# Four ring banks for the projections, one shared bank for all transposes, and a later split of a group's first weight chunk

## What is computed

```python
x = layernorm(x + mixer(x, ...))        # x is (16, 128, 256)
x = layernorm(x + xattn(x, ctx, ctx))   # 32 query heads, 8 key heads of size 8
x = layernorm(x + moe(x, ...))          # 8 experts, top 2, and a shared one

def mixer(x, W_in, conv_w, conv_b, A_log, D_param, dt_bias, W_out):
    proj = x @ W_in.T
    val, gate, Bp, Cp, dt = split(proj)      # 512, 512, 32*128, 32*128, 32
    val = silu(causal_conv(val, conv_w) + conv_b)
    dt = softplus(dt + dt_bias); ld = dt * -exp(A_log)
    # per head h: Y = (C B^T * exp(cum_l - cum_m), causal) @ val + D * val
    Y = Y * silu(gate)
    return Y @ W_out.T
```

## Time and profile before

| | us |
|---|---|
| median of 3 runs | 813.26 |
| lowest and highest | 808.52, 814.21 |
| the profiled execution, its own time | 812.88 |
| its span in the profile | 811.1 |

### The profile page before, as it was taken

How to read it: one execution, slowest core, us unless ns; L and a number is a source line. 1 busy time by engine, 2 the same in 40 slices (tenths; PEclk the granted TensorE clock), 3 DMA queues, 4 the chain that set the end, 5 groups by cost and what they waited for, 6 DMA issues and landing times. The chain is left out here.

```text
span 811.1 us, 17004 instructions
## 1 busy us (share of the span) xinstructions
PE 738.9 (91%) x5786; PEld 401.0 (49%) x5791; DVE 598.5 (74%) x1037; ACT 432.8 (53%) x781; POOL 370.0 (46%) x408
## 2 busy tenths in 40 slices
PE   6699999999999999999999999997799998686673
PEld 2355565555655555555555565665134443333342
DVE  4578767687686786776767778885788898449995
ACT  5665445754444664544575544554277887532333
POOL 5466337463453583433749637633023212115672
PEclk9799999999999999999999999999699999798997
DMA  7355421227423132542223533220230000034401
GB/s 262 97 168 169 104 51 54 65 50 126 134 52 87 43 78 52 168 103 49 54 58 84 98 72 67 62 45 1 95 112 22 21 22 21 0 127 167 151 26 52
DMA packets 35509, 66.28 MB, mean 82 GB/s; under 512 B 7121, under 2 KB 12113, under 8 KB 33873
## 3 DMA queue, kind: packets, MB, share of 16 engines
q1 hardware_dynamic: 34896, 65.28, 30.0%
q10 hardware_dynamic: 576, 0.56, 0.2%
HBM read 62.49 MB, written 2.42 MB: 80 GB/s over the span
## 5 line engine op out<-in xcount | busy, mean ns | idle before, releaser
L280 POOL TENSOR_TENSOR cum_rows<-cum_rows,cum_t 128x512 f32<-128x512 f32 x128 | 136.4, 1076 | 195.4 <-DMA cum_rows<-cum_scratch 195.4
L758 PE MATMUL pring<-xt_hi,w_hi 128*128 (+1 forms) x576 | 173.5, 383 | 11.5 <-DVE conv_h L647 6.8
L758 PE MATMUL pring<-xt_lo,w_hi 128*128 (+1 forms) x576 | 172.8, 382 | 0.0
L758 PE MATMUL pring<-xt_hi,w_lo 128*128 (+1 forms) x576 | 172.7, 382 | 0.0
L626 DVE TENSOR_TENSOR bt<-pring,bt 128x512 f16<-128x512 f32 x128 | 88.1, 688 | 74.1 <-ACT bt L434 74.0
L434 ACT CAST bt<-pring 128x512 f16<-128x512 f32 x128 | 74.6, 583 | 116.8 <-PE pring L758 116.8
L630 DVE TENSOR_TENSOR ct<-pring,ct 128x512 f16<-128x512 f32 x128 | 88.2, 689 | 55.6 <-ACT ct L438 55.3
L797 PEld LDWEIGHTS pscore<-ct,bt 128*128 128x128 f16 x1536 | 95.9, 98 | 34.7 <-issue 7.2
L797 PE MATMUL pscore<-ct,bt 128*128 128x128 f16 x1536 | 106.7, 219 | 2.9 <-DVE mt L598 2.2
L438 ACT CAST ct<-pring 128x512 f16<-128x512 f32 x128 | 74.8, 584 | 54.8 <-PE pring L758 54.8
L1089 DVE TENSOR_REDUCE mx<-bank_at 128x4 f32<-128x512 f32 x128 | 83.5, 689 | 14.0 <-PE bank_at L1165 13.0
(11 more groups left out here) (154 smaller groups left out, 944.2 us busy)
## 6 DMA issues: line engine op xcount, KB each, us to landing
cum_rows<-cum_scratch SPq DMA_DIRECT2D x32, 1024.0 KB, 8.0
w_raw<-in_w_in SPq DMA_DIRECT2D x34, 256.0 KB, 7.1
weight_b<-weight_scratch SPq DMA_DIRECT2D x8, 1024.0 KB, 6.5
q_rows<-in_xt SPq DMA_DIRECT2D x4, 512.0 KB, 6.1
acc<-in_x SPq DMA_DIRECT2D x1, 2048.0 KB, 7.6
vals<-in_vals SPq DMA_DIRECT2D x16, 128.0 KB, 2.0
out<-acc SPq DMA_DIRECT2D x4, 512.0 KB, 2.9
w_raw_e<-in_w_up SPq DMA_DIRECT2D x1, 1024.0 KB, 4.8
```

Source lines behind the costliest of these rows:

```text
L280: nc.gpsimd.tensor_tensor(rows[:, par, :, q], rows[:, par, :, q], own, ALU.subtract).then_inc(sem("since"), 1)
L758: mm = nc.tensor.matmul(bank[name][:], w[:, c, k, cols], x[:, k, bass.ds(n % TB, 1), :].rearrange("p o n -> p (o n)"), start=(i == 0), sto ...
```

## The change

The ring of three banks becomes one of four. T leaves the ring: the transposed values, the turned sums and all turned queries share a new bank, `pturn`, and `pdt` becomes another name of `py`. `turn_sums` of the later token blocks now waits for `pad_values(0)`, `turn_values` of step 15 for the queries of step 14, and `turn_q(b)` waits for `evac_q(b - 1)` where it waited for `evac_q(b - 2)`. In a refill step, `hi_part(refill, 0)` moves behind `evac_b(n, 0)`, `evac_c(n, 0)` and `decays(n, 0)`. No instruction of work is added or removed.

```diff
--- before.py
+++ after.py
@@ -123,23 +123,25 @@
         stats = sb("stats0", [P, NB, 6], F32)
         block_mv = sb("block_mv0", [P, NB, 2], F32)
 
-        pring = [ps(f"pring{i}", [P, TOK]) for i in range(3)]
+        RING = 4
+        pring = [ps(f"pring{i}", [P, TOK]) for i in range(RING)]
         pscore = [ps(f"pscore{i}", [P, TOK]) for i in range(2)]
-        pcum = ps("pcum", [P, TB, NB, H])
+        pturn = ps("pturn", [P, TOK])
+        pcum = pturn[:].rearrange("p (t b h) -> p t b h", t=TB, b=NB)
         py = ps("py", [P, TOK])
-        pdt = ps("pdt", [P, TOK])
-        turned = [pcum[:].rearrange("p t b h -> p (t b h)").bitcast(F16).rearrange("p (i n) -> p i n", n=L),
-                  pdt[:].bitcast(F16).rearrange("p (i n) -> p i n", n=L)]
-
-
-        order = ["val", "gate", "B0", "C0", "B1", "C1", "B2", "C2", "O0", "O1", "B3", "C3", "T"]
+        pdt = py
+        turned = pturn[:].bitcast(F16).rearrange("p (i n) -> p i n", n=L)
+
+
+        order = ["val", "gate", "B0", "C0", "B1", "C1", "B2", "C2", "O0", "O1", "B3", "C3"]
         order += [f"{k}{s}" for s in range(4, SLOTS) for k in "BC"]
-        bank = {name: pring[i % 3] for i, name in enumerate(order)}
-        assert len(order) % 3 == 0
+        bank = {name: pring[i % RING] for i, name in enumerate(order)}
+        assert len(order) % RING == 0
+        bank["T"] = pturn
 
         def consumed(eng, name, n):
 
-            i = order.index(name) - 3
+            i = order.index(name) - RING
             m = n if i >= 0 else n - 1
             was = order[i % len(order)]
             if was == "val":
@@ -150,10 +152,8 @@
                 eng.wait_ge(sem("b_evac"), 8 * m + int(was[1]) + 2)
             elif was[0] == "C":
                 eng.wait_ge(sem("c_evac"), 8 * m + int(was[1]) + 3)
-            elif was[0] == "O":
+            else:
                 eng.wait_ge(sem("acc_add"), 2 * m + int(was[1]) + 1)
-            else:
-                eng.wait_ge(sem("val_pad"), m + 2)
 
         mean_var, rstd, expo = moments
 
@@ -439,7 +439,7 @@
 
             def evac_q(b):
                 act.wait_ge(sem("q_turn_mm"), b + 1)
-                nc.scalar.copy(q_rows[:, b].rearrange("p t g n -> p (t g) n"), turned[b % 2]).then_inc(sem("q_rows"), 1)
+                nc.scalar.copy(q_rows[:, b].rearrange("p t g n -> p (t g) n"), turned).then_inc(sem("q_rows"), 1)
 
             def silus(n):
                 act.wait_ge(sem("gate_proj"), n + 1)
@@ -482,11 +482,11 @@
 
             def step(n, refill=None, queries=()):
                 silus(n)
-                if refill is not None:
-                    hi_part(refill, 0)
                 evac_b(n, 0)
                 evac_c(n, 0)
                 decays(n, 0)
+                if refill is not None:
+                    hi_part(refill, 0)
                 evac_b(n, 1)
                 high_y(n)
                 if refill is not None:
@@ -782,6 +782,8 @@
             def turn_sums(t0, t1):
                 if t0 == 0:
                     pe.wait_ge(sem("in_early"), 48)
+                else:
+                    pe.wait_ge(sem("val_pad"), 2)
                 for t in range(t0, t1):
                     pe.wait_ge(sem("dt_cum"), t + 1)
                     nc.tensor.transpose(pcum[:, t].rearrange("p b h -> p (b h)"), dz[:, 0, t * L:t * L + L], ident[:]).then_inc(sem("cum_turned"), 1)
@@ -824,8 +826,10 @@
                                                   wo_parts[:, pw, bass.ds(grp_prev(n), 1), :].rearrange("p o m -> p (o m)"), start=(i == 0), stop=(i == 2))
                     mm.then_inc(sem("out_mm"), 1)
 
-            def turn_values(n):
-                consumed(pe, "T", n)
+            def turn_values(n, queries=0):
+                pe.wait_ge(sem("val_pad"), n + 1)
+                if queries:
+                    pe.wait_ge(sem("q_rows"), queries)
                 pe.wait_ge(sem("val_silu"), n + 2)
                 for b in range(NB):
                     mm = nc.tensor.transpose(bank["T"][:, b * L:b * L + L], val_t[:, b * L:b * L + L], ident[:])
@@ -860,10 +864,11 @@
             def turn_q(b):
 
                 pe.wait_ge(sem("q_split"), 2 * b + 2)
-                if b >= 2:
-                    pe.wait_ge(sem("q_rows"), b - 1)
+                pe.wait_ge(sem("val_pad"), min(STEPS - 2 + b // 4, STEPS - 1) + 2)
+                if b >= 1:
+                    pe.wait_ge(sem("q_rows"), b)
                 for i in range(8):
-                    mm = nc.tensor.transpose(turned[b % 2][:, i, :], q_parts[:, b % 2, i].rearrange("p j c -> p (j c)"), ident16[:])
+                    mm = nc.tensor.transpose(turned[:, i, :], q_parts[:, b % 2, i].rearrange("p j c -> p (j c)"), ident16[:])
                 mm.then_inc(sem("q_turn_mm"), 1)
 
             def step(n, queries=()):
@@ -879,7 +884,7 @@
                     if s == 2:
                         out_project(n)
                     if s == 3:
-                        turn_values(n)
+                        turn_values(n, queries[0] if queries else 0)
                     if s == 5:
                         outputs(n, 0)
                     if 4 <= s < 4 + len(queries):
```

## The result

| | before | after |
|---|---|---|
| median, us | 813.61 (4 runs, 808.52 to 814.21) | 807.79 (4 runs, 806.69 to 809.03) |
| profiled execution, span | 812.88, 811.1 | 809.03, 807.2 |

The ratio is 0.9935, 95% interval 0.9911 to 0.9958: 5.3 us faster, within the 1% that was called no change. In ten later runs the changed kernel's median was 806.91. The two profiled executions differ by 3.9 us; the one of after is the slowest of its four.

What follows compares the result with a forecast made beforehand. TensorE was taken to bound the mixer. From 812.88, less 2.0 (step 0), 1.8 (refill steps) and 1.2 (steps 14 and 15), plus 0.8 (mixer's end), came 808.7, stated as 809 us; range 806.5 to 811.

Steps and rivals of the forecast that it cites:

- Step 0: Mixer's first step: TensorE's waits shrink and the first `weigh` comes earlier; 2.0 us gained, bounds 1.0 and 3.1.
- The lower end: Step 0: B2 and C2 run at the low clock, so the first `weigh` comes only 1.0 us earlier.
- the upper end of 3.1: Step 0: by the walk of the queues, the first `weigh` comes at about 37.5 instead of 40.61.
- Rival B: Whole kernel: waits only move, refill steps lose what they gain, the end costs 0.8; 813.7 us, chance 0.14.
- Refill steps: Three mixer steps: earlier copies of B0 and C0 gain 0.6 us a step, 1.8 in all; bounds 0 and 3.1.
- rival A: Whole kernel: all gaps go, clock stays up in step 0, refill steps become ordinary; 805.5 us, chance 0.20.
- Ordinary steps: Nine of the mixer's sixteen steps: they show no gap before C0, so nothing is gained or lost.
- Steps 14 and 15: Mixer's last two steps: C0's waits of 0.54 and 0.66 us for the convolution go; 1.2 us gained, bounds 0 and 1.2.
- The mixer's end: Last query blocks: block 11's transpose waits for the copy of block 10; 0.8 us lost, bounds 0 and 1.0.
- rival C: Step 0: the clock stays low, making TensorE's work there 4.7 us longer; 817.4 us, chance 0.09.
- The signs listed beforehand: Step 0: C0 17.6, B1 23.2, `weigh` 37.5 to 39.5; refill step 33.2; no C0 wait in steps 14, 15.

Runs made afterwards that it cites:

- e2: The kernel before with only the first chunk's split moved behind the copies of B0 and C0; median 810.36 us, ratio to before 0.9980.
- e5: The changed kernel with ten matmuls of zeros added in TensorE's idle pieces of step 0; median 804.77 us.
- e6: The kernel before with eight matmuls of zeros added in step 0, six before C0 and two before the third scores; median 809.98 us.
- e1: The changed kernel with the first chunk's split put back to its old place; median 808.42 us, ratio to before 0.9965.
- e10: The changed kernel with ten matmuls of zeros in the idle pieces of step 0, run again; median 805.92 us.

## Why the prediction was right, and where its terms were off

The forecast was 808.7 to 809, within 1%; measured were 807.79 and 806.91. The sum came out by luck: the term of step 0 was too high by 2.4 us, and those of the refill and the ordinary steps too low by 1.5 and 0.8.

**Step 0 (2.0 gained).** Wrong in its sign in the traces: from the Tanh of `val` to the transpose of step 1 the profiled execution lost 0.4 us (52.42 against 52.00), and beside e2, the other trace of the old step 0, it lost 1.9. The step that failed is "I take the middle of 1.0 and 3.1". The lower end came true up to the first `weigh` (1.1 to 1.2), but I stopped the walk there: a third fall of the clock, behind the wait for that `weigh`, took it back. I had written that idle pieces of at most 2.2 us did not lower the clock; here one of the same 2.2 us was followed by a fall at 41. And the upper end of 3.1 was not to be had: at full clock the first `weigh` comes 1.9 us earlier than before (15.51 against 17.44), of which 0.5 is the ring's and the rest the clock's (e5, e6). Rival B's argument for step 0, that the waits only move, holds but for that half microsecond.

**Refill steps (1.8 gained).** The mechanism was right and e1 and e2 gave the expected halves, but the size was 33.78 - 32.66 = 1.1 each, 3.3 us in all: rival A's term. My walk gave each of ScalarE's operations its duration of 0.6 us, where consecutive ones start 0.52 apart (261.90, 262.42, 262.94). Over the operations up to it that put the copy of C1 0.5 us too late, which is the wait that I forecast and that did not come. The loss weighed against this term, GpSimd's chunk in the way of VectorE, did not come: the chunk ran from 263.13 to 264.29, behind the gating of y (262.40) and only 0.13 us into `val_silu` (264.16), which took 0.68 us each.

**Ordinary steps (nothing).** 0.04 us each in most, about 0.3 in all, and 0.5 in step 4, which went from 33.25 to 32.78; either change alone removes that too (e1 32.66, e2 32.70). I had read no gap in the starts; the weight loads had one at C0.

**Steps 14 and 15 (1.2 gained).** From the transpose of step 13 (471.19 before, 467.73 after) to that of step 15 it was 68.43 and is 67.55: 0.9 gained. Over all traces it is 68.43 to 68.77 with the ring of three (before, e2, e6) and 67.10 to 67.58 with the ring of four, so 0.9 to 1.7, around the forecast.

**The mixer's end (0.8 lost).** 0.35 in the first pair of traces, by the clock; the shared bank itself costs 0.9 at the full clock, which the walk assumed, and 1.3 at the low one. The chain of the copy of block 10, the transpose and the copy of block 11 is the one that was forecast.

**The chances.** Rival A was right on the refill steps, rival B nearly so on step 0, and rival C named the right thing, the clock, at a third of the size (1.6 us lost behind the first `weigh`, where it had 4.7): it fell three times but never stayed low. The signs listed beforehand came for C0, B1, the `weigh` (at the late end, 39.5), C0 of steps 14 and 15 and the last copy; the refill step of 33.2 us and "the low clock shorter than 10 us" (it was the same, in three pieces) did not.

Open is why the medians differ by 5.8 us where the first two traces differ by 3.9. That single executions of the same kernel differ by what the clock does in step 0 is shown (52.00 and 50.53 for before and e2); whether that makes up the rest is not.

## What to carry to other kernels

When a wait is moved, walk on until the engines are in step again; a gain read at the first meeting point can be gone at the next. Before two traces are compared, line them up at an event ahead of the change: here their starts differ by up to 0.8 us, more than the 0.5 that the ring wins in step 0. In a stage bound by TensorE, compare the intervals between equal instructions: 1.1 us every fourth step stood there plainly, while the list of waits showed 0.2. If two transposes and their copies share a bank at a stage's end, look for a bank that the stage has just left.

## What the runs showed of the hardware

TensorE's granted clock fell to 0.50 after an idle piece of 2.2 us in one trace (behind 41 in the changed kernel) and stayed at 1.00 after one of the same length in another (behind 41.45 in step 0 before), so a short wait can't be called safe from one trace. Matmuls of zeros in the idle pieces kept it at 1.00 from 20 to 60 (e5, e10), and cost nothing where they fitted (B1 of e5 at 23.30, as in the changed kernel). Consecutive ScalarE operations of 0.61 to 0.63 us started 0.52 us apart. A VectorE operation with two SBUF operands took 1.38 us when a GpSimd one had started 0.32 us before it (e5), and 0.68 alone; where it started first (e6), the GpSimd operation took 1.65 us in place of 1.15.
